# Cross-attention block on one core: the last output tile finished by column halves, and steps moved between ScalarE, VectorE and SyncE in the first and last batch

## The chip, the core and the metric

One NeuronCore of one Trainium2 chip. The metric is the device time of one execution in microseconds (us); lower is better. TensorE (PE) multiplies matrices into the accumulator banks (PSUM), VectorE (DVE), ScalarE (ACT) and GpSimd (POOL) work elementwise, and SyncE (SP) and ScalarE issue DMAs.

## The reference

```
x: (16, 100, 640)   ctx: (16, 722, 384) = enc (718 rows) + ca (4 rows)
query = x @ Wq;  keyt = enc @ Wk;  valt = enc @ Wv
hs = mha(query, keyt, valt)                      # 8 heads of 80
ca_q1 = einsum('btc,th->bch', ca, Wq_ca)[:, picked 100 rows]
ca_hs1 = mha(ca_q1, x, x)
ca_hs2 = mha(ca_hs1 @ Wq, ca @ Wk_ca, ca @ Wv_ca)
out = (hs + ca_hs2) @ Wout + b_out + x
```

Everything is float32. The kernel splits each operand of a product into a high and a low part in a type that TensorE takes at full rate and adds three products (high x high, high x low, low x high). So nearly every result comes as a pair of steps: ScalarE writes the high part (`..._high`), VectorE or GpSimd the low part (`..._low`), which is the value less its high part.

## The kernel before

The program has four stretches, and the order of the work in each is written out by hand, engine by engine; the engines meet in semaphores only. Each engine takes its own list in order, so an instruction that waits holds up all that stands behind it.

1. **Prologue.** `first_queries`, then `query(g, j)` for four column groups of x and `m_parts`, 40 small products per head and column block, written between the queries. `m_parts` for head h waits for the low part of that head's Wq (`head_low(h)`, semaphore hlo). VectorE makes them in order behind `weight_low(5, ...)`, the low part of Wk. SP's list issues the loads and the stores: `store_q` and `store_g` write the queries of group 0 back to DRAM, and the load of Wk stood behind them.
2. **`batch(0, first=True)`**, which has the queries of group 3 (`query(3, 0..5)`) written between its own steps. They all use one PSUM bank, `psB[:, 1]`, so `query(3, j)` waits for `q_low(3, j - 1)`. ScalarE also makes the high parts of Wv in it (`wv_high(0..2)`), and GpSimd subtracts them (`wv_low`).
3. **`batch(i)` for i = 1 to 14** in a loop, and `batch(15, last=True)`, which has no keys of a next batch and starts the output product instead: `tile(0, 0)`.
4. **The output tiles.** `tile(r, j)` makes 128 rows of out in 30 matmuls of 320 columns, in two column halves. 1600 rows are 12 tiles of 128 and one of 64, the last. `high(r, j)` (ACT) and `low(r, j)` (DVE) prepare its operand. `finish(r, j)` (DVE) adds the bias and the residual x, and `store(r, j)` (ACT) writes the rows out.

A batch on TensorE is, per head h: `scores` (product with the keys), `turn(h)` (transposes of the probabilities) and, per column block, `context(i, u)`. On VectorE `rowmax`, then ScalarE's `expo`, then `norm(i, h)` on VectorE, which scales the probabilities of a head by one over their sum: a reciprocal (L1593), a short copy of 39 columns (L1595) and the 718 columns themselves (L1599). `turn(i, h)` waits for `norm(i, h)` and for `pt_low(i, h - 1)`. `c2_copy`, `b2_less_max2` and `b2_norm2` (L1687 writes P2x) belong to the second, small attention, whose last transpose, `b2_turn2`, is L915.

Of the kernel before, what the change touches and what calls it, by code (L numbers as in the profile page):

```python
# [13 lines left out]
HEADS = 8  # L14
# [81 lines left out]
def program(nc, x, xT, encT, encN, caT, asel, Wq, WqT, Wk, Wv, WqcaBD, Wkca, Wvca, Wout, bout, out,  # L96
            q_d, g_d, v2_d, m_d, hs_d):

    with ExitStack() as ctx:
# [234 lines left out]
        with nc.Block() as block:  # L334
            @block.sync
            def _(sp):
# [401 lines left out]
            def _(pe):  # L738
# [179 lines left out]
                def tile(r, j, n=128, first=False):  # L918

                    pe.wait_ge(s["clo"], 2 * r + j + 1)  # L920
                    if first:
                        pe.wait_ge(s["wolo"], FT)
                        pe.wait_ge(s["exp"], HEADS * B)
                    else:
                        pe.wait_ge(s["csum"], 2 * r + j - 1)
# [7 lines left out]
                    mm.then_inc(s["cmm"], 1)  # L933
# [110 lines left out]
                def batch(i, first=False, last=False):  # L1044
# [120 lines left out]
            def _(act):  # L1165
# [10 lines left out]
                def pt_high(i, h, first=False):  # L1176
# [3 lines left out]
                    if first and h == 4:  # L1180
# [4 lines left out]
                        psT[0:KP, :, 0:3 * S].rearrange("p a (k n) -> p a k n", k=3), ACT.Copy).then_inc(s["pthi"], 1)  # L1185

# [159 lines left out]
                def batch(i, first=False, last=False):  # L1346
# [42 lines left out]
                    if first:  # L1389
                        q_high(3, 4)  # L1390
# [6 lines left out]
                    if first:  # L1397
                        xm_copy(i)
                        expo(i, 5)
# [25 lines left out]
                    if last:  # L1425
                        wo_high(3)
                        wo_high(4)
                        u_high(i, 0)
# [8 lines left out]
                    if first:  # L1437
                        wv_high(0)
                    b2_exp2(i)
                    if last:  # L1440
                        high(0, 0, first=True)
# [3 lines left out]
                    if first:  # L1445
                        wv_high(1)
# [4 lines left out]
                    if first:  # L1451
                        wv_high(2)
                    pt_high(i, 7)
                    if not last:
                        k_high(i + 1, 2)
                    if last:
# [123 lines left out]
                store(FULL // 2, 0, REST)  # L1580
                act.wait_ge(s_st[0], 16 * (FULL // 2 + 1))
# [3 lines left out]
            def _(dve):  # L1585
# [5 lines left out]
                def norm(i, h):  # L1591
# [8 lines left out]
                                            None, ALU.mult).then_inc(s["norm"], 1)  # L1600

# [101 lines left out]
                def finish(r, j, n=128, first=False):  # L1703
                    dve.wait_ge(s["cmm"], 2 * r + j + 1)
# [285 lines left out]
```

## Time and profile before

| | |
|---|---|
| device time, median of 3 runs | 985.36 us (984.73 to 988.87) |
| the profiled execution | 982.17 us |
| its span, first to last instruction | 980.5 us |
| PE busy in the span | 962.7 us (98%) |
| DVE, ACT, POOL busy | 708.7, 491.8, 343.5 us |
| granted PE clock, mean | 0.998 |

The busy times are sums over the span. PE is at work nearly all the time, so what it waits for, where, and how long, is what the profile has to answer; the times of the other engines matter only where PE waits for them.

### The profile page before, as it was taken

The numbers are of one execution on the slowest core, as the hardware profiler recorded it, in microseconds if no ns is written. First come the engines' busy times: TensorE is split into PE (matmuls) and PEld (weight loads), VectorE is DVE, ScalarE is ACT, GpSimd is POOL, SyncE is SP. The second block draws the span as 40 slices with busy tenths as digits, with TensorE's granted clock in tenths as the row PEclk, the third lists the DMA queues.
The fourth block names the chain that finished last, engine by engine and source line by source line (L and its number), as shares of the span: only waits on it lengthen the run. The fifth ranks groups of instructions, "written<-read, shape, count | busy, mean of one in ns | idle before, by whom it ended". The sixth has DMA issues, their size and how long they took to land.

```text
span 980.5 us, 21024 instructions
## 1 busy us (share of the span) xinstructions
PE 962.7 (98%) x6644; PEld 942.8 (96%) x6644; DVE 708.7 (72%) x1257; ACT 491.8 (50%) x911; POOL 343.5 (35%) x302
## 2 busy tenths in 40 slices
PE   9999989999999999999999999999999999998998
PEld 8998889999999999999999999999999999998997
DVE  6455687777777778787777877777777777777444
ACT  6434545455555546464646363736464545455110
POOL 5223353434342516161615252433433433424000
PEclk9999999999999999999999999999999999999999
DMA  7899967797979787978797979787887878795364
GB/s 264 267 294 267 291 158 209 179 212 175 210 178 203 185 200 187 191 192 193 198 186 199 189 196 183 209 188 200 184 212 166 223 168 212 177 226 156 102 193 141
DMA packets 157545, 195.21 MB, mean 199 GB/s; under 512 B 81040, under 2 KB 111568, under 8 KB 157520
## 3 DMA queue, kind: packets, MB, share of 16 engines
q1 hardware_dynamic: 150000, 181.53, 75.4%
q10 hardware_dynamic: 7520, 13.35, 4.5%
q8 instruction: 15, 0.25, 0.1%
q14 instruction: 10, 0.08, 0.0%
HBM read 82.74 MB, written 19.95 MB: 105 GB/s over the span
## 4 chain that ended last, share of the span: by engine, by line
PE 87%; DVE 5%; DMA 4%; ACT 2%; SPq 1%; issue 0%; ACTq 0%
PE psS L780 22%; PE psB L815 17%; PE psB L820 9%; PE psS L755 8%; PE psT L796 6%; PE psS L930 6%; PE psT L848 4%; PE psT L854 2%; PE psB L825 2%; PE psB L827 2%; DMA g_split<-PT_l 1%; PE psB L880 1%; PE psB L903 1%; PE psT L855 1%; PE psB L965 1%; DVE probs L1599 1%
## 5 line engine op out<-in xcount | busy, mean ns | idle before, releaser
L780 PE MATMUL psS<-encT_keep,Wk_keep 128*128 128x360 f32 x1440 | 254.1, 330 | 0.0
L780 PEld LDWEIGHTS psS<-encT_keep,Wk_keep 128*128 128x128 f32 x1440 | 237.8, 189 | 0.7
L1172 ACT ACTIVATE probs<-psS,negmax 100x718 f32<-100x718 f32 x128 | 110.2, 861 | 132.7 <-DVE negmax L1588 132.6
L815 PE MATMUL psB<-PT_h,encN_h 128*128 128x400 f32 x480 | 169.5, 353 | 0.0
L815 PE MATMUL psB<-PT_l,encN_h 128*128 128x400 f32 x480 | 165.7, 345 | 0.0
L635 POOL TENSOR_TENSOR encT_keep<-encT_raw,encT_keep 128x718 fp32r<-128x718 f32 x45 | 83.5, 1856 | 170.1 <-ACT encT_keep L1201 165.5
L1605 DVE TENSOR_TENSOR PT_l<-psT,PT_h 128x600 fp32r<-128x600 f32 x128 | 99.5, 777 | 38.3 <-ACT PT_h L1183 35.0
L626 POOL TENSOR_TENSOR Mbd<-Mbd,fmask 128x320 fp32r<-128x320 f32 x48 | 43.1, 898 | 220.1 <-DMA Mbd<-m_split 217.5
L1588 DVE TENSOR_REDUCE negmax<-psS 100x1 f32<-100x720 f32 x128 | 114.6, 895 | 0.1
L1599 DVE TENSOR_SCALAR probs<-probs,inv 100x718 f32<-100x718 f32 x128 | 106.6, 833 | 4.5
L1183 ACT ACTIVATE PT_h<-psT 128x600 fp32r<-128x600 f32 x128 | 85.7, 669 | 44.8 <-PE psT L796 42.4
L820 PE MATMUL psB<-PT_h,encN_l 128*128 128x400 f32 x480 | 103.8, 346 | 0.5 <-POOL encN_l L650 0.5
L1621 DVE TENSOR_TENSOR UT<-psB,UT 128x400 fp32r<-128x400 f32 x96 | 55.0, 573 | 64.7 <-ACT UT L1225 64.7
L1196 ACT ACTIVATE kT<-psS 128x718 fp32r<-128x718 f32 x80 | 61.6, 770 | 79.3 <-PE psS L780 76.6
L1225 ACT ACTIVATE UT<-psB 128x400 fp32r<-128x400 f32 x96 | 48.2, 502 | 92.1 <-PE psB L827 92.1
L1616 DVE TENSOR_TENSOR kT<-psS,kT 128x718 fp32r<-128x718 f32 x80 | 72.0, 900 | 27.4 <-ACT kT L1196 26.1
L815 PEld LDWEIGHTS psB<-PT_h,encN_h 128*128 128x128 f32 x480 | 90.4, 188 | 0.4
L815 PEld LDWEIGHTS psB<-PT_l,encN_h 128*128 128x128 f32 x480 | 90.5, 188 | 0.0
L796 PE MATMUL psT<-ident,probs 100*128 100x100 f32 x768 | 87.0, 249 | 2.8 <-DVE PT_l L1605 2.2
L820 PEld LDWEIGHTS psB<-PT_h,encN_l 128*128 128x128 f32 x480 | 88.1, 188 | 1.1 <-POOL encN_l L650 1.1
L755 PE MATMUL psS<-kstack,qstack_h 120*100 120x360 f32 x256 | 87.9, 343 | 0.3 <-DMA kstack<-kT 0.3
L796 PEld LDWEIGHTS psT<-ident,probs 100*128 100x128 f32 x768 | 79.3, 140 | 7.9 <-issue 2.8
(253 smaller groups left out, 1791.9 us busy)
## 6 DMA issues: line engine op xcount, KB each, us to landing
kstack<-kT SPq DMA_DIRECT2D x64, 448.8 KB
kstack<-kT SPq DMA_DIRECT2D x192, 112.2 KB
enc_raw<-in_encN_dram SPq DMA_DIRECT2D x48, 384.0 KB, 4.6
encT_raw<-in_encT_dram SPq DMA_DIRECT2D x45, 359.0 KB, 5.1
kstack<-kT SPq DMA_DIRECT2D x32, 359.0 KB
kstack<-kT SPq DMA_DIRECT2D x32, 269.2 KB
kstack<-kT SPq DMA_DIRECT2D x32, 179.5 KB, 3.6
kstack<-kT SPq DMA_DIRECT2D x64, 89.8 KB, 3.9
```

Of the source, the lines that this page charges most:

```text
L635: nc.gpsimd.tensor_tensor(eT[1][:, c, :], rawT[:, c, :], eT[0][:, c, :], ALU.subtract).then_inc(s["encT"], 1)
L755: mm = pe.matmul(psS[score_slot[h]][0:S, half, 0:HALF], qst[p][:, h, :], kst[:, p, h % SLOTS, k0:k0 + HALF], start=(p == 0), stop=(p == 1))
L780: mm = pe.matmul(keys_in(f, first)[:, half, 0:HALF], w[:, c, f * 128:(f + 1) * 128], e[:, c, k0:k0 + HALF], start=(j == 0), stop=(j == 3 * ...
L796: mm = pe.transpose(psT[0:KP, k // 3, (k % 3) * S:(k % 3 + 1) * S], P[h % PRING][0:S, k * KP:(k + 1) * KP], ident[0:S, 0:S])
L815: pe.matmul(psB[:, 1, 0:RH], eN[0][:, k, cc], PT[p][:, k, rows], start=(k == 0 and p == 0), stop=False)
L820: pe.matmul(psB[:, 1, 0:RH], eN[1][:, k, cc], PT[0][:, k, rows], start=False, stop=False)
L1172: nc.scalar.activation(halves(P[h % PRING][0:S, 0:KEYS]), without_overlap(psS[score_slot[h]], S), ACT.Exp, bias=negmax[:, h:h + 1], accum_ ...
L1183: nc.scalar.activation(PT[0][:, :, h * S:(h + 1) * S].rearrange("p (a k) n -> p a k n", a=2), psT[0:KP, :, 0:3 * S].rearrange("p a (k n) - ...
L1588: nc.vector.tensor_reduce(negmax[:, h:h + 1], tile_in(h), AX.XY, ALU.max, negate=True).then_inc(s["negmax"], 1)
L1599: nc.vector.tensor_scalar(P[h % PRING][0:S, 0:KEYS], P[h % PRING][0:S, 0:KEYS], inv[:, h:h + 1], None, ALU.mult).then_inc(s["norm"], 1)
L1605: nc.vector.tensor_tensor(o[1], psT[0:KP, :, 0:3 * S].rearrange("p a (k n) -> p a k n", k=3), o[0], ALU.subtract).then_inc(s["ptlo"], 1)
L1616: nc.vector.tensor_tensor(halves(kT[f % 2][1][:, :]), without_overlap(keys_in(f, first), 128), halves(kT[f % 2][0][:, :]), ALU.subtract).t ...
```

## The change

Seven edits:

- Prologue, SP: the load of Wk is issued ahead of `store_q(0, ...)`, and `store_g(0)` behind the load of heads 3 to 5.
- Prologue, DVE: the sum `k2_sum` is made ahead of the two `v2` subtractions.
- First batch: `query(3, 4)` stands behind `turn(0, 3)` and `scores(0, 5)` on PE; `rowmax(0, 5)` and `expo(0, 5)` stand further forward on DVE and ACT.
- First batch, ACT: `wv_high(0)` and `wv_high(1)` stand behind `b2_pt2_high`, `wv_high(2)` behind `k_high(1, 2)`.
- Last batch: `norm(15, 5)` and `norm(15, 6)` run on ScalarE, with the scale taken from `inv`; VectorE keeps their reciprocals (`one_over`). `high(0, 0)` and `low(0, 0)` stand further forward.
- `finish` adds bias and x before it waits for the product, and adds the product then; `tile` waits for the second of these steps (cres) instead of the first (csum).
- The last tile (64 rows) signals after each column half, and is finished and stored in two halves.

```diff
                 load_heads(0, 3)
+                sp.wait_ge(s["wlo"], 4)
+                sp.dma_start(wk_raw, tiled(Wk)).then_inc(s["wkin"], 16)
                 store_q(0, 0, 3)
                 store_q(0, 3, FT)
-                store_g(0)
-                sp.wait_ge(s["wlo"], 4)
-                sp.dma_start(wk_raw, tiled(Wk)).then_inc(s["wkin"], 16)
                 sp.wait_ge(s["hlo"], 3)
                 load_heads(3, 3)
+                store_g(0)
...
-                        pe.wait_ge(s["csum"], 2 * r + j - 1)
+                        pe.wait_ge(s["cres"], 2 * r + j - 1)
...
-                    mm.then_inc(s["cmm"], 1)
+                        if half == 1 or n < 128:
+                            mm.then_inc(s["cmm"], 1)
...
                     b2_turn(i, 1)
-                    if first:
-                        query(3, 4)
-                    else:
+                    if not first:
                         context(i - 1, 5)
                     turn(i, 3)
                     scores(i, 5)
+                    if first:
+                        query(3, 4)
...
+                def norm(i, h):
+                    act.wait_ge(s["inv"], 2 * (HEADS * i + h) + 1)
+                    nc.scalar.activation(P[h % PRING][0:S, KEYS:KEYS + TH],
+                                         P[h % PRING][0:S, FULLK * KP:FULLK * KP + TH], ACT.Copy,
+                                         scale=inv[:, h:h + 1]).then_inc(s["inv"], 1)
+                    act.wait_ge(s["inv"], 2 * (HEADS * i + h) + 2)
+                    nc.scalar.activation(P[h % PRING][0:S, 0:KEYS], P[h % PRING][0:S, 0:KEYS], ACT.Copy,
+                                         scale=inv[:, h:h + 1]).then_inc(s["norm"], 1)
...
+                def one_over(i, h):
+                    dve.wait_ge(s["exp"], HEADS * i + h + 1)
+                    dve.wait_ge(s["inv"], 2 * (HEADS * i + h))
+                    nc.vector.reciprocal(inv[:, h:h + 1], total[:, h:h + 1]).then_inc(s["inv"], 1)
...
                 def finish(r, j, n=128, first=False):
-                    dve.wait_ge(s["cmm"], 2 * r + j + 1)
                     if not first:
                         dve.wait_ge(s_st[j], 16 * r)
                     v = [halves(t[0:n, 0:H]) for t in (res[j], bias, xin[j])]
-                    nc.vector.tensor_tensor(v[0], psS[j][0:n, :, 0:HW], v[1], ALU.add).then_inc(s["csum"], 1)
+                    dve.wait_ge(s_x[j], 16 * r + 16)
+                    nc.vector.tensor_tensor(v[0], v[1], v[2], ALU.add).then_inc(s["csum"], 1)
                     dve.wait_ge(s["csum"], 2 * r + j + 1)
-                    dve.wait_ge(s_x[j], 16 * r + 16)
-                    nc.vector.tensor_tensor(v[0], v[0], v[2], ALU.add).then_inc(s["cres"], 1)
+                    if n == 128:
+                        dve.wait_ge(s["cmm"], 2 * r + j + 1)
+                        nc.vector.tensor_tensor(v[0], psS[j][0:n, :, 0:HW], v[0], ALU.add).then_inc(s["cres"], 1)
+                    else:
+                        for half in range(2):
+                            dve.wait_ge(s["cmm"], 2 * r + j + 1 + half)
+                            nc.vector.tensor_tensor(v[0][:, half, :], psS[j][0:n, half, 0:HW], v[0][:, half, :],
+                                                    ALU.add).then_inc(s["cres"], 1)
```

The other moves have no line that says more than the list. Three places of the order:

SP's queue in the prologue, from the load of Wv_ca on (`probs<-in_WqT_dram` are the heads' rows of Wq, `encT_raw<-in_Wk_dram` is Wk):

```order
 L424 DMA probs<-in_WqT_dram 80x3x640
+L463 DMA encT_raw<-in_Wk_dram 128x3x640
 L435 DMA q_split<-PT_h 128x3x400
 L435 DMA q_split<-PT_l 128x3x400
 L435 DMA q_split<-PT_h 128x2x400
 L435 DMA q_split<-PT_l 128x2x400
+L424 DMA probs<-in_WqT_dram 80x3x640
 L442 DMA g_split<-PT_h 64x400
 L442 DMA g_split<-PT_l 32x400
-L466 DMA encT_raw<-in_Wk_dram 128x3x640
-L424 DMA probs<-in_WqT_dram 80x3x640
```

Wk moved ahead of six stores, the heads ahead of two.

ScalarE at the end of the first batch, before (from `pt_high(0, 5)`; `Wv_h` is written by `wv_high`, `P2T` by `b2_pt2_high`, `kT` by `k_high`):

```order
L1183 ACTIVATE PT_h<-psT 128x6x100
L1324 ACTIVATE Wv_h<-encT_raw 128x640
L1253 ACTIVATE P<-P 100x32
L1196 ACTIVATE kT<-psS 128x718
L1324 ACTIVATE Wv_h<-encT_raw 128x640
L1183 ACTIVATE PT_h<-psT 128x6x100
L1257 ACTIVATE P2T<-psB 96x100
L1324 ACTIVATE Wv_h<-encT_raw 128x640
L1183 ACTIVATE PT_h<-psT 128x6x100
L1196 ACTIVATE kT<-psS 128x718
```

and of the change:

```order
L1184 ACTIVATE PT_h<-psT 128x6x100
L1263 ACTIVATE P<-P 100x32
L1206 ACTIVATE kT<-psS 128x718
L1184 ACTIVATE PT_h<-psT 128x6x100
L1267 ACTIVATE P2T<-psB 96x100
L1334 ACTIVATE Wv_h<-encT_raw 128x640 x2
L1184 ACTIVATE PT_h<-psT 128x6x100
L1206 ACTIVATE kT<-psS 128x718
L1334 ACTIVATE Wv_h<-encT_raw 128x640
```

The first Wv copy stands four instructions later, the last one behind the keys' high part.

ScalarE in the last batch, before (from the copy of hs; `Wk_keep<-encT_raw` is `wo_high`, the high part of Wout, `UT` is `u_high(15, 0)`):

```order
L1230 ACTIVATE hs<-psT 80x400
L1262 ACTIVATE Wk_keep<-encT_raw 128x640 x2
L1225 ACTIVATE UT<-psB 128x4x100
L1183 ACTIVATE PT_h<-psT 128x6x100
L1172 ACTIVATE probs,total<-psS,negmax 100x718
```

and of the change:

```order
L1240 ACTIVATE hs<-psT 80x400
L1190 ACTIVATE probs<-probs,inv 100x39
L1194 ACTIVATE probs<-probs,inv 100x718
L1272 ACTIVATE Wk_keep<-encT_raw 128x640 x2
L1190 ACTIVATE probs<-probs,inv 100x39
L1194 ACTIVATE probs<-probs,inv 100x718
L1235 ACTIVATE UT<-psB 128x4x100
L1184 ACTIVATE PT_h<-psT 128x6x100
L1173 ACTIVATE probs,total<-psS,negmax 100x718
```

Four instructions came in ahead of the copy of UT.

## Rows read from the trace of the kernel before

In rows of busy time stand start:end and length in us, then busy us (and instructions) of PE, PEld (TensorE's weight loads), DVE, ACT and POOL, the granted PE clock (1.00 is full), the DMA engines' busy share and GB/s.

**Rows 1.** Busy time of each engine by stretch of the span

```profile
0.00:60.00 60.00, 56.14 (x343) 53.68 (x344) 32.08 (x46) 32.39 (x56) 24.98 (x41) 0.97 0.87 273
60.00:140.00 80.00, 73.55 (x447) 69.14 (x447) 50.44 (x87) 38.33 (x72) 27.37 (x23) 1.00 0.88 248
140.00:880.00 740.00, 739.99 (x5207) 729.35 (x5206) 572.74 (x1045) 394.83 (x737) 276.57 (x229) 1.00 0.83 195
880.00:906.00 26.00, 23.15 (x170) 21.48 (x169) 19.62 (x37) 15.20 (x32) 14.59 (x10) 1.00 0.58 168
```

**Rows 2.** Timeline of PE, prologue: start, us, what [idle before and its releaser]

```profile
30.37 1.50 PE L1039 MATMUL psS<-kstack,P1T 80*128 80x64 f32 x12 [0.57 <-issue]
...
42.21 1.52 PE L1039 MATMUL psS<-kstack 80*128 80x64 f32 x12 [1.19 <-DVE kstack L1743]
```

**Rows 3.** Busy time and clock behind that gap

```profile
45.00:49.00 4.00, 4.00 (x18) 3.98 (x16) 0.12 (x1) 0.26 (x1) 3.69 (x5) 0.57 0.84 250
```

**Rows 4.** Chain of waits, prologue: start, us, what

```profile
29.91 7.50 DMA encT_raw<-in_Wk_dram
...
37.43 1.82 ACT Wk_keep L1294
...
39.27 2.16 DVE Wk_keep L1732
```

**Rows 5.** Timeline of PE, first batch

```profile
111.11 0.42 PE L965 MATMUL psB<-encN_h,Wv_h 128*128 128x400 f32 x1 [1.41 <-DVE PT_l L1737]
...
133.06 0.29 PE L915 MATMUL psB<-ident,P2x 100*96 100x100 f32 x1 [1.12 <-DVE P2x L1687]
...
138.25 0.71 PE L796 MATMUL psT<-ident,probs 100*128 100x100 f32 x6 [1.90 <-DVE PT_l L1605]
```

**Rows 6.** Timeline of DVE, end of the first batch

```profile
131.44 1.57 DVE L1687 TENSOR_TENSOR P2x<-P,st 100x96 f32<-100x96 f32 x1
...
133.11 1.50 DVE L1595 TENSOR_SCALAR probs<-probs,inv 100x39 f32<-100x39 f32 x1
134.64 1.96 DVE L1599 TENSOR_SCALAR probs<-probs,inv 100x718 f32<-100x718 f32 x1
```

**Rows 7.** Timeline of GpSimd, same place

```profile
131.35 4.85 POOL L672 TENSOR_TENSOR Wv_l<-encT_raw,Wv_h 128x640 fp32r<-128x640 f32 x3
```

**Rows 8.** Timeline of DVE, last batch

```profile
890.23 1.96 DVE L1599 TENSOR_SCALAR probs<-probs,inv 100x718 f32<-100x718 f32 x1
...
895.30 1.65 DVE L1599 TENSOR_SCALAR probs<-probs,inv 100x718 f32<-100x718 f32 x1
...
898.62 0.26 DVE L1687 TENSOR_TENSOR P2x<-P,st 100x96 f32<-100x96 f32 x1
...
898.98 0.24 DVE L1595 TENSOR_SCALAR probs<-probs,inv 100x39 f32<-100x39 f32 x1
899.26 0.59 DVE L1599 TENSOR_SCALAR probs<-probs,inv 100x718 f32<-100x718 f32 x1
```

**Rows 9.** Timeline of PE, last batch

```profile
893.67 0.73 PE L796 MATMUL psT<-ident,probs 100*128 100x100 f32 x6 [0.55 <-DVE P L1665]
...
900.65 0.41 PE L930 MATMUL psS<-Wk_keep,kT 128*128 128x320 f32 x1 [1.54 <-DVE kT L1700]
```

**Rows 10.** Timeline of ACT, last batch

```profile
888.82 1.36 ACT L1262 ACTIVATE Wk_keep<-encT_raw 128x640 fp32r<-128x640 f32 x2
891.24 0.50 ACT L1225 ACTIVATE UT<-psB 128x400 fp32r<-128x400 f32 x1 [1.06 <-PE psB L827]
...
894.47 0.86 ACT L1172 ACTIVATE probs<-psS,negmax 100x718 f32<-100x718 f32 x1 [2.04 <-DVE negmax L1588]
```

**Rows 11.** Timeline of DVE, end of the program

```profile
975.88 0.82 DVE L1708 TENSOR_TENSOR encT_raw<-psS,enc_raw 64x640 f32<-64x640 f32 x1 [2.71 <-PE psS L930]
976.73 0.82 DVE L1711 TENSOR_TENSOR encT_raw<-encT_raw 64x640 f32<-64x640 f32 x1
```

**Rows 12.** A DVE operation of half that width, by line: count, busy, mean ns

```profile
L1871 DVE TENSOR_TENSOR qstack_l<-psS,qstack_h 64x320 fp32r<-64x320 f32 x2 | 0.9, 471 | 0.0
```

More of the change, by code:

```diff
@@ L1389, in batch @@
                     if first:
+                        expo(i, 5)
                         q_high(3, 4)
@@ L1425, in batch @@
                     if last:
+                        norm(i, 5)
                         wo_high(3)
                         wo_high(4)
+                        norm(i, 6)
                         u_high(i, 0)
@@ L1436, in batch @@
                     pt_high(i, 5)
-                    if first:
-                        wv_high(0)
+                    if last:
+                        high(0, 0, first=True)
                     b2_exp2(i)
                     if last:
-                        high(0, 0, first=True)
                         u_high(i, 1)
@@ L1451, in batch @@
                     if first:
-                        wv_high(2)
+                        wv_high(0)
+                        wv_high(1)
                     pt_high(i, 7)
@@ L1455, in batch @@
                         k_high(i + 1, 2)
+                    if first:
+                        wv_high(2)
                     if last:
@@ L1579, in _ @@
                 store(FULL // 2 - 1, 1)
-                store(FULL // 2, 0, REST)
-                act.wait_ge(s_st[0], 16 * (FULL // 2 + 1))
+                for half in range(2):
+                    act.wait_ge(s["cres"], FULL + 1 + half)
+                    act.dma_start(out2[FULL * 128:NT, half * HW:(half + 1) * HW],
+                                  res[0][0:REST, half * HW:(half + 1) * HW]).then_inc(s_st[0], 16)
+                act.wait_ge(s_st[0], 16 * (FULL // 2 + 2))
                 act.wait_ge(s_st[1], 16 * (FULL // 2))
@@ L1785, in batch @@
                     b2_pt_low(i, 1)
+                    if first:
+                        rowmax(i, 5)
                     norm(i, 4)
@@ L1791, in batch @@
                     if first:
-                        rowmax(i, 5)
                         xm_add(i)
@@ L1806, in batch @@
                         xm_low(i)
+                    if last:
+                        one_over(i, 5)
                     if not first:
                         hs_add(i - 1, 1)
-                    norm(i, 5 if first or last else 6)
+                    if last:
+                        one_over(i, 6)
+                    else:
+                        norm(i, 5 if first else 6)
                     if last:
@@ L1816, in batch @@
                     rowmax(i, 7)
-                    if first or last:
+                    if first:
                         norm(i, 6)
@@ L1822, in batch @@
                     pt_low(i, 5)
+                    if last:
+                        low(0, 0)
                     b2_norm2(i)
@@ L1825, in batch @@
                     if last:
-                        low(0, 0)
                         u_low(i, 1)
@@ L1867, in _ @@
                 head_low(2)
+                dve.wait_ge(s["k2hi"], 3)
+                k2_parts = psB[0:D, :, :].rearrange("d b (h a n) -> d b h a n", h=4, a=2)
+                k2_sum4 = k2_sum.rearrange("d (b h n) -> d b h n", b=2, h=4)
+                nc.vector.tensor_tensor(k2_sum4, k2_parts[:, :, :, 0, :], k2_sum4, ALU.add).then_inc(s["k2lo"], 1)
                 for j in range(2):
```

8 lines of the change are left out of this document (1 added, 7 removed).

## The prediction

> **What bounds the kernel now.** I read the busy times by stretch first, because they say where TensorE stands still. From 140 to 880 us, the fourteen looped batches, PE is busy for 739.99 of 740 us [rows 1]: nothing can be gained there, and whatever PE is early by at 140 it keeps, unless a wait comes up that was not there. The other stretches have all the slack there is: 3.86 us in the first 60 us, 6.45 us from 60 to 140, 2.85 us from 880 to 906 [rows 1], and what follows the last product. So I went through PE's timeline in these stretches, gap by gap, and for each gap through the timeline of the engine that released it, and in the prologue the chain of waits.
>
> In the prologue PE waits 0.57 us ahead of the first small products and 1.19 us ahead of those of head 3 [rows 2]. The chain behind the second: the load of Wk starts at 29.91 and takes 7.50 us, ScalarE's copy of it starts at 37.43, VectorE's subtraction runs 2.16 us from 39.27, and only then comes the head's low part [rows 4]. A little after that gap the granted clock falls: over 45 to 49 us its mean is 0.57 with PE busy all the time [rows 3], 4.00 x 0.43 = 1.72 us of work lost at the lower of the two rates (1.2 instead of 2.4 GHz).
>
> In the first batch PE waits 1.41 us for `query(3, 4)`, 1.12 us for P2x and 1.90 us for `turn(0, 7)` [rows 5]. The last two have one source: on VectorE the P2x step takes 1.57 us, the short copy 1.50 and the long one 1.96 us [rows 6], where the same three take 0.26, 0.24 and 0.59 us late in the last batch [rows 8]. During the slow ones GpSimd runs the three Wv subtractions, 4.85 us from 131.35 on [rows 7]. In the last batch the same long copy takes 1.96 and 1.65 us [rows 8], and PE waits 0.55 us for `c2_copy` and 1.54 us for `low(0, 0)` [rows 9].
>
> **The change part by part.**
>
> *Prologue.* Wk's load needs `weight_low(4)`, done about when SP issues its first store, and then has the 2 MB of query stores behind it instead of ahead. With its 7.50 us [rows 4] kept it lands near 31 instead of 37.4; then heads 3 to 5, issued some 3 us earlier, decide. Head 3's low part was ready at about 42.2, the moment PE goes on [rows 2], and now is ready some 3 to 4 us earlier, so the 1.19 us gap closes. The bound from the other side: if the DMA engines are so full that the heads land as late as before, Wk's 1.82 and 2.16 us are at least out of the line, and about 1 us remains. `store_g(0)` lands later; `q_high(1, 0)` waits for it, but stands behind head 3 on ScalarE anyway. `k2_sum` ahead of two subtractions of 0.47 us [rows 12] brings the last `k2` step forward by about 0.45 of the 0.57 us. If the gap is gone I take the slow clock to be gone too: 0.45 + 1.19 + 1.72 = 3.36 us, between 1.0 and 3.36.
>
> On this last term the Trainium skill, page "TensorE: Matmul & The Clock Gate", Part 1, says that idling brings the slow rate on and that the watch over activity runs freely and does not restart with the kernel, so that one kernel shows different numbers of slow matmuls from run to run. By that rule this stretch may stay although the gap closes, and the sum would be 1.7 us less; or other gaps pay for one in other runs.
>
> *First batch, `query(3, 4)`.* It cannot start before `q_low(3, 3)`, at 111.11 [rows 5], wherever it stands. The transposes and scores, ten short matmuls of some 1.2 us, now fill the wait ahead of it, and no longer stand between it and `query(3, 5)`, which has to wait for `q_low(3, 4)`: about 1.4 us from the end of one to the start of the next, with some 0.8 us of `b2_xm` in it. So 1.2 us gained, 0.6 to 0.7 paid again: net 0.5 us, between 0.2 and 1.2.
>
> *First batch, Wv.* GpSimd's subtractions cannot start before the high parts, which now follow `b2_pt2_high`, 2.3 us later. By then P2x and the two copies of `norm(0, 7)` are through: 1.31 + 1.26 + 1.37 = 3.94 us shorter on VectorE [rows 6, 8]. The P2x gap of 1.12 goes to 0.0 to 0.1; `pt_low(0, 6)` is then done 0.5 us before PE comes to `turn(0, 7)`, so the 1.90 goes too: 3.0 us. What is late next is GpSimd: its last subtraction ends about 139.3 on the old scale, and PE, now 3.2 us ahead, wants Wv at 140.4. That is 1.1 us of cover; each further us of delay costs one.
>
> *Last batch.* VectorE's work between `hs_add` and `u_low` falls by both norms' copies. On ScalarE a copy with a scale read per row is not in the trace; the nearest row, the exponential with a bias read per row on the same 718 columns, takes 0.86 us [rows 10]. The short one lies between nothing and that; I take 0.3. Each pair holds ScalarE some 1.1 us, less overlap. With the two Wout copies of 1.36 us [rows 10] between them, the copy of UT, which started at 891.24 [rows 10], starts about 892.3, and `pt_high`, `pt_low` and `c2_copy` follow it: the 0.55 us gap [rows 9] grows to about 1.35. Behind it VectorE has no `norm` left and `low(0, 0)` is ready at 898.3, while PE is there at 899.2: the 1.54 us gap [rows 9] closes, and a short one before `turn(15, 6)`. So tile 0 starts at 899.2 instead of 900.65: 1.4 us gained; 0.5 if the copies take 0.4 us more each than I think.
>
> *Output tiles.* In all but the last tile there is still one VectorE step between the product and the release of its bank, so PE sees no change. The bias and x sum now waits for x before the bank is released, but x is loaded a whole tile ahead. At the end two steps follow the last matmul, from 975.88 to 977.55 [rows 11]. Now only one of half the width does: a half-width operation took 0.471 us [rows 12]. 1.69 - 0.49 = 1.2 us gained. The first half's store is hidden behind the matmuls.
>
> Sum: 3.36 + 0.5 + 3.0 + 1.4 + 1.2 = 9.5 us. The profiled execution took 982.17, so 972.7 us like that one. The median of the runs is 985.36, 3.2 us above it; I put the same gain there: 985.4 - 9.5 = 975.9.
>
> **The rivals.** A difference under 0.5% (4.9 us) is about what a measurement of this kernel can't tell from none.
>
> 1. *The prologue's gain is not kept* (the heads land as before, or the slow clock comes anyway). For it: the DMA share is 0.87 in the first 60 us and 0.88 in the next 80 [rows 1], so transfers crowd. Against it: PE released nearly all that followed in the old chain. Price: 1.7 to 2.4 us, so 977.6 to 978.3.
> 2. *The copies stay stretched, or Wv comes late.* A Wv subtraction takes a third of 4.85, 1.62 us [rows 7], and a stretched copy 1.26 to 1.37 us more than a free one [rows 6, 8], as if it waited out most of one. If the first subtraction starts before `norm(0, 7)` is through, one copy waits, and PE by up to 1.6 us; or GpSimd is the one held up, and PE waits for Wv before the loop. Up to 3.0 us lost: 978.9. The margin is 0.9 us by the rows. The Trainium skill, page "SBUF — State Buffer", section "SBUF: two separate sides", has a rule for it: the port pair that VectorE and GpSimd share is an exclusive lock, held by whoever starts first for its whole instruction.
> 3. *Both, or most of prologue and first batch absorbed before 140 us.* Then 2.6 to 4 us are left: 981.4 to 982.8, within the noise.
> 4. *More than forecast.* The unprofiled runs are 2.6 to 6.7 us slower than the profiled one. If that is one or two more slow-clock stretches at the gaps of the first batch, they go with the gaps: 1.7 or 3.4 us more, 972.5 to 974.2.
> 5. *Slower.* `csum`, which opens `finish`, now waits for the load of x, and the bank's release stands behind it. If that load landed late, PE would wait at each of some nine tiles. An x load is issued a little over 4 us before VectorE could use it and the bank is wanted a tile (4.4 us) after that. To undo 9.5 us and cost 5 more, each would have to be late by 1.6 us beyond both margins: 990. It decides when a load takes over about 8 us.
>
> **How the numbers follow.** Forecast 0.47, rival 1 0.18, rival 2 0.10, rival 4 0.09, rival 3 0.13, rival 5 0.03. The first four, 0.84, end under 980.4 and are "faster by over 0.5%"; the third 0.13, "within"; the fifth 0.03, "slower". The likeliest case gives 975.9. The range leaves out the far half of rival 4, most of rival 3's upper end and rival 5: 972 to 981.5.
>
> **What would show it.** In the profile after: no gap before head 3's products and no lower clock between 40 and 50 us; Wk's copy on ScalarE near 30 instead of 37.43; P2x, short and long copy at the end of the first batch near 0.26, 0.24 and 0.59; GpSimd's Wv steps starting after them and PE not waiting for Wv; PE starting tile 0 about 9 us earlier than 900.65, with a longer wait before the `turn` that follows `c2_copy`; two scaled copies on ScalarE near 0.9 us; one half-width step of 0.47 us after the last matmul. The prediction is wrong if the stretch from 140 on starts less than 4 us earlier than before, or if a new wait stands at the start of the loop.

## The result, and the profile after

| | before | after |
|---|---|---|
| median of 13 runs each | 984.73 us (980.34 to 989.39) | 975.57 us (971.92 to 980.56) |
| ratio | | 0.9909, 95% interval 0.9890 to 0.9928 |
| the profiled execution, its span | 982.17, 980.5 us | 975.57, 973.9 us |

The changed kernel is 9.2 us faster by the medians; 9.5 had been forecast. The profiled executions are only 6.6 us apart.

Busy time by stretch of the changed kernel, columns as in [rows 1]:

```profile
0.00:60.00 60.00, 58.27 (x354) 56.01 (x355) 34.16 (x49) 34.60 (x60) 24.76 (x41) 0.97 0.88 275
60.00:140.00 80.00, 76.58 (x458) 72.27 (x456) 48.44 (x90) 37.23 (x69) 27.47 (x23) 0.98 0.92 257
140.00:880.00 740.00, 740.00 (x5210) 729.18 (x5210) 571.35 (x1045) 397.46 (x742) 278.36 (x230) 1.00 0.83 194
...
33.00:37.00 4.00, 4.00 (x17) 3.97 (x16) 0.08 (x1) 0.13 (x1) 0.00 (x0) 0.57 1.06 313
94.00:99.00 5.00, 4.50 (x16) 4.46 (x17) 3.41 (x5) 2.05 (x5) 0.00 (x0) 0.66 0.88 224
```

PE's idle time fell from 3.86 to 1.73 us in the first 60 us and from 6.45 to 3.42 us in the next 80. The last two rows are what the forecast's sum had not counted and rival 1 had named. The lower clock, the 1.2 GHz level, which stood at 45 to 49 us [rows 3], is at 33 to 37 now and again at 94 to 99. Each costs 4.00 x 0.43 or 5.00 x 0.34, about 1.7 us.

PE's timeline, the gaps of the first and the last batch:

```profile
82.15 0.38 PE L755 MATMUL psS<-kstack,qstack_h 120*100 120x360 f32 x1 [0.59 <-DMA kstack<-kT]
93.04 0.41 PE L755 MATMUL psS<-kstack,qstack_h 120*100 120x360 f32 x1 [0.81 <-DVE kT L1636]
...
111.53 0.42 PE L966 MATMUL psB<-encN_h,Wv_h 128*128 128x400 f32 x1 [0.44 <-DVE PT_l L1763]
115.79 0.91 PE L939 MATMUL psB<-encN_h,v2bd 128*64 128x400 f32 x4 [0.47 <-DVE PT_l L1763]
...
131.50 0.27 PE L915 MATMUL psB<-ident,P2x 100*96 100x100 f32 x1
134.64 0.68 PE L796 MATMUL psT<-ident,probs 100*128 100x100 f32 x6
...
891.01 0.73 PE L796 MATMUL psT<-ident,probs 100*128 100x100 f32 x6 [1.46 <-DVE P L1685]
895.71 0.39 PE L930 MATMUL psS<-Wk_keep,kT 128*128 128x320 f32 x1
```

Against [rows 5, 9]: 1.41 us became 0.44 and a new 0.47; the gaps of 1.12, 1.90 and 1.54 us are gone; 0.55 grew to 1.46. VectorE at the end of the first batch, and the first two of GpSimd's three Wv steps:

```profile
131.17 0.26 DVE L1707 TENSOR_TENSOR P2x<-P,st 100x96 f32<-100x96 f32 x1
...
131.53 0.24 DVE L1610 TENSOR_SCALAR probs<-probs,inv 100x39 f32<-100x39 f32 x1
131.81 0.59 DVE L1614 TENSOR_SCALAR probs<-probs,inv 100x718 f32<-100x718 f32 x1
...
133.43 3.22 POOL L672 TENSOR_TENSOR Wv_l<-encT_raw,Wv_h 128x640 fp32r<-128x640 f32 x2 [2.42 <-ACT Wv_h L1334]
```

The three steps have the lengths of [rows 8] instead of those of [rows 6], and GpSimd starts behind them. ScalarE in the last batch with the two copies that it took over, and VectorE at the end of the program:

```profile
885.28 0.32 ACT L1190 ACTIVATE probs<-probs,inv 100x39 f32<-100x39 f32 x1
885.63 0.90 ACT L1194 ACTIVATE probs<-probs,inv 100x718 f32<-100x718 f32 x1
...
888.83 0.48 ACT L1235 ACTIVATE UT<-psB 128x400 fp32r<-128x400 f32 x1
```

```profile
967.33 0.81 DVE L1728 TENSOR_TENSOR encT_raw<-enc_raw,encT_raw 64x640 f32<-64x640 f32 x1
968.78 0.48 DVE L1736 TENSOR_TENSOR encT_raw<-psS,encT_raw 64x320 f32<-64x320 f32 x1 [0.64 <-PE psS L930]
970.91 0.48 DVE L1736 TENSOR_TENSOR encT_raw<-psS,encT_raw 64x320 f32<-64x320 f32 x1 [1.65 <-PE psS L930]
```

Where the 6.6 us lie, by the starts of the same instructions on PE:

| | before | after | ahead by |
|---|---|---|---|
| `keys(0, 0)`, the first key product | 62.20 | 60.32 | 1.88 |
| `keys(1, 0)` | 118.43 | 118.29 | 0.14 |
| `b2_turn2` of batch 0 | 133.06 | 131.50 | 1.56 |
| `b2_turn2` of batch 1 | 186.12 | 182.62 | 3.50 |
| tile 0 | 900.65 | 895.71 | 4.94 |
| last matmul | 975.53 | 970.56 | 4.97 |
| end of the span | 980.5 | 973.9 | 6.6 |

Between 60 and 118 us the lead was lost again: 1.71 us to the second slow stretch (a stretch at the lower clock), 0.7 us to waits that vary from run to run, against the 0.7 us that `query(3, 4)` gave.

### The profile page after: what moved, and what is told of

It reads as the page before. It is cut to its first block, busy times and chain, and to the rows that moved or that the text cites. A ratio compares the mean times of both kernels' runs of the same rounds, so it can differ in the third digit from the quotient of the medians.

```text
span 973.9 us, 21030 instructions
## 1 busy us (share of the span) xinstructions
PE 963.8 (99%) x6644; PEld 944.6 (97%) x6644; DVE 700.7 (72%) x1254; ACT 494.4 (51%) x915; POOL 342.3 (35%) x302
## 4 chain that ended last, share of the span: by engine, by line
PE 91%; DVE 2%; ACT 2%; DMA 2%; SPq 1%; POOL 1%; issue 1%; ACTq 0%; POOLq 0%
PE psS L780 24%; PE psB L815 18%; PE psB L820 9%; PE psS L755 8%; PE psT L796 6%; PE psS L930 6%; PE psT L848 4%; PE psT L854 2%; PE psB L966 2%; PE psB L825 2%; PE psB L827 2%; PE psS L1040 1%; PE psB L880 1%; PE psB L903 1%; PE psT L855 1%; PE psT L966 1%
## 5 line engine op out<-in xcount | busy, mean ns | idle before, releaser
L635 POOL TENSOR_TENSOR encT_keep<-encT_raw,encT_keep 128x718 fp32r<-128x718 f32 x45 | 83.6, 1858 | 177.6 <-ACT encT_keep L1211 173.2
L1614 DVE TENSOR_SCALAR probs<-probs,inv 100x718 f32<-100x718 f32 x126 | 101.2, 803 | 4.4
L1206 ACT ACTIVATE kT<-psS 128x718 fp32r<-128x718 f32 x80 | 61.7, 771 | 83.6 <-PE psS L780 76.4
```

The costliest lines, as they stand in the source:

```text
L635: nc.gpsimd.tensor_tensor(eT[1][:, c, :], rawT[:, c, :], eT[0][:, c, :], ALU.subtract).then_inc(s["encT"], 1)
L1614: nc.vector.tensor_scalar(P[h % PRING][0:S, 0:KEYS], P[h % PRING][0:S, 0:KEYS], inv[:, h:h + 1], None, ALU.mult).then_inc(s["norm"], 1)
```

## The experiments

Twelve more kernels ran, the changed one again among them, in three sets, each on one chip beside the kernel before. Each run also lists its mean granted clock.

| kernel | runs | median, us | ratio to before (95%) | mean clock |
|---|---|---|---|---|
| before, set 1, 2, 3 | 35, 29, 17 | 985.00, 983.94, 984.89 | | 0.9953, 0.9963, 0.9959 |
| after, the first runs (beside 13 of before, 984.73) | 13 | 975.57 | 0.9909 (0.9890 to 0.9928) | 0.9979 |
| e1_prologue (set 1) | 12 | 984.37 | 0.9993 (0.9970 to 1.0015) | 0.9959 |
| e2_wv (1) | 12 | 983.19 | 0.9984 (0.9966 to 1.0002) | 0.9951 |
| e3_last (1) | 12 | 984.43 | 0.9990 (0.9968 to 1.0012) | 0.9954 |
| e5_gp (1) | 12 | 981.15 | 0.9975 (0.9952 to 0.9998) | 0.9957 |
| after_again (2) | 6 | 976.25 | 0.9933 (0.9909 to 0.9957) | 0.9983 |
| e6_one_piece (2) | 12 | 978.62 | 0.9943 (0.9921 to 0.9965) | 0.9968 |
| e7_norm6 (2) | 12 | 976.69 | 0.9934 (0.9909 to 0.9958) | 0.9977 |
| e9_g2 (2) | 12 | 978.49 | 0.9941 (0.9921 to 0.9961) | 0.9970 |
| e10_two (3) | 6 | 979.54 | 0.9946 (0.9924 to 0.9967) | 0.9977 |
| e12_first (3) | 12 | 982.09 | 0.9972 (0.9955 to 0.9988) | 0.9959 |
| e11_old_q34 (3) | 6 | 978.09 | 0.9923 (0.9897 to 0.9949) | 0.9962 |
| e14_best (3) | 6 | 976.81 | 0.9919 (0.9892 to 0.9946) | 0.9975 |

A part of the change is worth one to three us, and an interval is some 4 us wide. So each part is read from the trace, stretch by stretch, and the times serve as a check. Where the clock's share is said to be taken off a time, that is the time less (1 - clock) x span, run by run, and the means are compared.

**e1_prologue: the prologue's edits alone.**

```diff
+                sp.wait_ge(s["wlo"], 4)
+                sp.dma_start(wk_raw, tiled(Wk)).then_inc(s["wkin"], 16)
                 store_q(0, 0, 3)
...
                 load_heads(3, 3)
+                store_g(0)
```

> The kernel before with the two prologue edits alone (load of Wk ahead of the query stores, store_g(0) behind the heads, k2_sum earlier). Theory A, the gain is the closed waits and nothing else: the gaps of 0.57 and 1.19 us on TensorE are gone, what follows stands 1.8 to 1.9 us earlier, and a stretch of lower clock, some 3.4 us long, still comes somewhere in the first 100 us, since the changed kernel showed two of them with the gap closed: 1.8 us less than before. Theory B, as the prediction had it, the lower clock belongs to the gap before head 3: no stretch below full clock in the first 60 us, 3.4 us less than before. Theory C, the early load of Wk crowds out the later transfers and the gain is paid back before 140 us: 0 to 0.5 us less than before, with longer waits for kstack's rows or for the keys' high part between 80 and 95 us.

Both gaps are gone and the first key product starts at 58.70, 1.8 us earlier than before's with its slow stretch taken off. The stretch of lower clock that theory A also expected in the first 100 us did not come; this trace has none before its end. But PE's timeline has this further on, which is what theory C had named:

```profile
82.08 0.38 PE L755 MATMUL psS<-kstack,qstack_h 120*100 120x360 f32 x1 [1.76 <-DMA kstack<-kT]
```

By tile 0 nothing of the lead is left: 899.23 against 900.65 - 1.71 = 898.94 before. By the times the edits gave 0.6 us, and 0.4 with the clock's share taken off. In e10_two beside e12_first, which differ by the same edits, it is 2.6 us by the medians and 0.6 with that share off. What they are worth beside the clock is within the noise of the times; it takes several traces. The first key product, each slow stretch ahead of it taken off at 1.71 us, starts on average at 58.9 in the nine traces with these edits (58.6 to 59.3) and at 60.05 in the five without them (59.5 to 60.5): 1.1 us. At `keys(0, 3)`, near 84 us, it is still 1.0 (83.6 against 84.6). The wait of 1.76 us is this trace's alone: the other eight with the edits have 0 to 0.6 us there, the five without 0 to 0.65. The gap before head 3 is 1.19 us in [rows 2], but 0.89, 0.65 and 0.25 us in e2_wv, e3_last and e12_first, and e5_gp's timeline has none. Theory A holds for the closed gaps, not for the size. Theory C's longer wait does not repeat; how much of the 1.1 us the program keeps to its end no run settles. Theory B fits this one trace and falls by the others: with the gap closed the low clock still came ahead of 38 us in five of the nine traces, both of the changed kernel's among them; of the five without the edits two have it ahead of 50 us.

**e2_wv and e12_first: Wv alone, and the first batch alone.** e2_wv moves only the Wv copies; e12_first has `query(3, 4)`, `rowmax(0, 5)` and `expo(0, 5)` at their new places as well.

```diff
-                    if first:
-                        wv_high(0)
                     b2_exp2(i)
...
                     b2_pt2_high(i)
+                    if first:
+                        wv_high(0)
+                        wv_high(1)
```

> The kernel before with wv_high(0..2) moved to their new places and nothing else. Theory A, the three long copies on VectorE were held up by GpSimd's Wv subtractions beside them: P2x step, short copy and long copy take 0.26, 0.24 and 0.59 us, the gaps of 1.12 and 1.90 us on TensorE go, nothing waits for Wv, 3.0 us less than before. Rival, the gain belongs to TensorE being 2.4 us ahead through the other edits: with Wv moved alone a Wv subtraction still meets one of the copies, one of them stays above 1.3 us, and 1 to 2 us are gained.

> The kernel before with the first batch's edits alone (Wv and query(3, 4) with rowmax and expo). Theory A, Wv alone had given 2.1 us behind P2x, with 0.97 us of a new wait ahead of turn(0, 6) in place of the 1.12 us for P2x, since norm(0, 6) now met GpSimd's next two steps full on (1.25 and 1.92 us in place of 0.38 and 1.64); query(3, 4) gives 0.7 and moves that meeting: 2.8 us less than before if norm(0, 6) is still met full on, 3.5 to 4 if not. Rival, the two edits don't touch each other: 0.7 + 2.1 = 2.8 with the wait of 0.97 unchanged.

In e2_wv the three steps take 0.26, 0.25 and 0.60 us and the gap before `turn(0, 7)` is gone, but only 2.1 us are gained: the wait for P2x came back one transpose earlier. PE, VectorE and GpSimd of e2_wv:

```profile
131.68 0.71 PE L796 MATMUL psT<-ident,probs 100*128 100x100 f32 x6 [0.97 <-DVE PT_l L1604]
```

```profile
126.54 1.25 DVE L1594 TENSOR_SCALAR probs<-probs,inv 100x39 f32<-100x39 f32 x1
127.83 1.92 DVE L1598 TENSOR_SCALAR probs<-probs,inv 100x718 f32<-100x718 f32 x1
```

```profile
126.51 1.24 POOL L620 TENSOR_TENSOR xTb_l<-P,xTb_h 128x500 fp32r<-128x500 f32 x1
127.83 1.52 POOL L602 TENSOR_TENSOR gbd<-g_in,headmask 128x800 fp32r<-128x800 f32 x1
```

`norm(0, 6)` met two other GpSimd steps full on: the short copy ends 0.04 us behind the first of them, the long one 0.40 us behind the second. In the kernel before it met these steps at another phase, with 0.38 and 1.64 us. In e12_first the same copies take 0.25 and 1.65 us, no wait stands at `turn(0, 6)`, and from `keys(1, 0)` to `b2_turn2` of batch 1 it takes 64.57 us, against 67.69 before and 65.57 in e2_wv. With the 0.7 us of `query(3, 4)` that is 3.8 us, as theory A had it for a norm that is not met full on; the times say 2.8 us, with an interval of 1.2 to 4.4.

That it is `query(3, 4)` which avoids the meeting is not shown. e11_old_q34 has it at its old place and avoids the meeting too: 0.47 and 1.65 us, no wait, 64.31 us for the stretch. e6_one_piece and e9_g2 have it at the new place and meet GpSimd all but full on, with waits of 0.67 and 0.81 us ahead of `turn(0, 6)`. VectorE in e9_g2:

```profile
125.43 1.09 DVE L1610 TENSOR_SCALAR probs<-probs,inv 100x39 f32<-100x39 f32 x1
126.56 1.92 DVE L1614 TENSOR_SCALAR probs<-probs,inv 100x718 f32<-100x718 f32 x1
```

So `query(3, 4)` is worth 0.7 us, and up to 1 us of the gain of the Wv edit hangs on a phase that varies from trace to trace and that these runs don't trace to one edit.

**e5_gp: GpSimd held back, ScalarE left alone.**

```diff
                 spread_g(1)
+                pool.wait_ge(s["norm"], HEADS)
                 wv_low()
```

> The kernel before with one more wait: GpSimd begins its three Wv subtractions only when the first batch's last norm(0,7) is done; ScalarE's copies of Wv stay where they were. Theory A, GpSimd's subtractions are what stretches VectorE's three steps: they take 0.26, 0.24 and 0.59 us here too, the gaps of 1.12 and 1.90 us go; with nothing paid back 3.0 us less than before, and up to 1 us of it paid if TensorE then waits for Wv. Rival, ScalarE's copies of Wv beside them, or the traffic of transfers, stretches them: they stay at 1.3 to 2.0 us and the time is that of before.

VectorE and GpSimd:

```profile
131.10 0.26 DVE L1688 TENSOR_TENSOR P2x<-P,st 100x96 f32<-100x96 f32 x1
...
131.47 0.25 DVE L1596 TENSOR_SCALAR probs<-probs,inv 100x39 f32<-100x39 f32 x1
131.75 0.60 DVE L1600 TENSOR_SCALAR probs<-probs,inv 100x718 f32<-100x718 f32 x1
```

```profile
132.49 4.85 POOL L672 TENSOR_TENSOR Wv_l<-encT_raw,Wv_h 128x640 fp32r<-128x640 f32 x3 [2.93 <-ACT Wv_h L1325]
```

ScalarE's copies of Wv still run beside the three steps and do no harm. GpSimd's steps were the cause; the rival falls. With one wait more the program is 3.85 us faster by the medians; in the trace it gains the same 2.1 us in this stretch as e2_wv and has, likewise, 0.95 us of wait ahead of `turn(0, 6)`.

**e3_last: the last batch alone.**

```diff
+                        norm(i, 5)
                         wo_high(3)
                         wo_high(4)
+                        norm(i, 6)
                         u_high(i, 0)
```

> The kernel before with the edits of the last batch alone (heads 5 and 6 normalised on ScalarE, high(0,0) and low(0,0) further forward). Theory A: the gap before low(0,0)'s tile (1.54 us) goes, the one behind c2_copy grows from 0.55 to 1.4 to 1.5 us, tile 0 starts 1.4 us earlier measured from the gap of 0.42 us at the start of this batch; 1.4 us less than before, too small for the time alone to tell. Rival, the 1.4 us in the changed kernel came in part from its being 3.5 us ahead of the loads: then under 0.7 us here.

From the small gap of 0.42 us at the start of this batch to tile 0 it takes 13.88 us (887.65 to 901.53), against 15.19 before (885.46 to 900.65) and 13.79 in the changed kernel. 1.3 to 1.4 us, with the gap behind `c2_copy` at 1.37: theory A. The times alone, 0.6 us less, could not have told.

**after_again.**

> The changed kernel once more, on the chip and in the rounds of the next three. Its first 13 runs had a mean granted clock of 0.9979, while 35 runs of the kernel before, and 48 of the kernels with one part of the change each, had 0.9951 to 0.9959. Theory A, with all the waits closed the low clock comes less often: 0.997 to 0.998 here against 0.995 to 0.996 of before beside it, 9.0 to 9.5 us less than before, of which some 6.5 to 7 us is work and waits and 2 to 2.5 us the clock. Theory B, the difference in clock belonged to the chip or the hour: both clocks within 0.0005 of each other here and 6.5 to 8.3 us less than before.

7.7 us less by the medians, clock 0.9983 against 0.9963. The clock is theory A's, the time is within theory B's bounds; the interval, 4.2 to 9.0 us, reaches into both. With the clock's share taken off it is 5.7 us, less than the 6.5 to 7 that theory A gave to work and waits. The clock's difference came again with the two kernels side by side, so chip and hour alone don't explain it. Its ScalarE and PE show a wait that the prediction had not named:

```profile
123.37 0.67 ACT L1184 ACTIVATE PT_h<-psT 128x600 fp32r<-128x600 f32 x1 [2.25 <-DMA g_split<-PT_l]
```

```profile
126.97 3.23 PE L780 MATMUL psS<-encT_keep,Wk_keep 128*128 128x360 f32 x18 [0.71 <-ACT probs L1173]
```

`pt_high(0, 4)` writes where `query(3, 5)` was kept and waits until that is stored. It did so before the change too (0.41 us). Over the thirteen traces with it the wait is 0.31 to 4.34 us, and the store takes 4.3 to 8.2 us from issue to landing. `pt_high(0, 4)` is followed on ScalarE by `expo(0, 7)`, and PE waits for that.

**e6_one_piece: the last tile in one piece, in the new order.**

```diff
-                    if n == 128:
-                        dve.wait_ge(s["cmm"], 2 * r + j + 1)
-                        nc.vector.tensor_tensor(v[0], psS[j][0:n, :, 0:HW], v[0], ALU.add).then_inc(s["cres"], 1)
-                    else:
-                        for half in range(2):
...
+                    dve.wait_ge(s["cmm"], 2 * r + j + 1)
+                    nc.vector.tensor_tensor(v[0], psS[j][0:n, :, 0:HW], v[0], ALU.add).then_inc(s["cres"], 1)
```

> The changed kernel with its last tile finished and stored in one piece; the order bias + x first, product last is kept. Of the 1.63 us that the end gained in the profile, 1.20 was VectorE's and 0.43 the store's. Theory A: behind the last product stand one step of 0.82 us and a store of 2.9 us, so the end is 0.34 + 0.43 = 0.8 us later than in the changed kernel, and the reordering alone is worth the other 0.85. Rival, the store takes 2.5 us at either size: 0.35 us later. Both are read from the last rows of the profile; the time is 0.4 to 0.8 us above that of the changed kernel.

```profile
977.18 0.81 DVE L1727 TENSOR_TENSOR encT_raw<-psS,encT_raw 64x640 f32<-64x640 f32 x1 [2.84 <-PE psS L930]
```

From that step's end, 977.99, to the end of the span of 980.9 it is 2.9 us; before, 980.5 - 977.55 = 2.95; in the changed kernel, 973.9 - 971.39 = 2.5. Theory A: of the end's 1.6 us, 0.86 come from the order of the sums (975.88 to 977.55 [rows 11] became one step of 0.81), 0.33 from the half-width step and 0.4 from the smaller store.

**e7_norm6: head 6 normalised behind `pt_high(15, 4)`.**

```diff
                         wo_high(4)
-                        norm(i, 6)
                         u_high(i, 0)
...
                     pt_high(i, 4, first)
+                    if last:
+                        norm(i, 6)
                     expo(i, 7)
```

> The changed kernel with norm(15, 6) on ScalarE behind pt_high(15, 4) instead of ahead of u_high(15, 0). Theory A, the gap of 1.46 us behind c2_copy is made by that norm standing ahead of the copy of UT, 1.2 us in ScalarE's queue: UT's copy starts about 1.1 us earlier, the gap shrinks to 0.4 to 0.5 us, tile 0 starts 1.0 us earlier, 1.0 us less than the changed kernel. Rival, head 6's normalisation is now late for turn(15, 6), or VectorE's own steps set the place of c2_copy: the gap only moves, 0 to 0.3 us gained.

```profile
894.62 0.73 PE L796 MATMUL psT<-ident,probs 100*128 100x100 f32 x6 [0.46 <-ACT probs L1194]
```

The gap is 0.46 us and tile 0 starts 12.77 us behind the 0.42 us gap instead of 13.79: 1.0 us, theory A. The profiled run lost more elsewhere, and the median is not below after_again's. ScalarE in its first batch:

```profile
126.22 0.67 ACT L1184 ACTIVATE PT_h<-psT 128x600 fp32r<-128x600 f32 x1 [4.34 <-DMA g_split<-PT_l]
```

**e9_g2: `store_g2` issued behind `k_high(0, 3)`.**

```diff
                         store_q2(4, FT)
-                        store_g2()
...
                         q_high(3, 0)
+                        store_g2()
```

> The changed kernel with store_g2 issued behind k_high(0, 3) and q_high(3, 0) instead of ahead of them. In its trace ScalarE spends 0.80 and 2.26 us issuing these two stores (0.57 and 1.25 in the kernel before), the keys' high part starts right behind them at 91.27, and TensorE waits 0.81 us for their low part. Theory A, the wait of 0.81 us is those issues': it goes, k_high stands 2 us earlier, and 0.5 to 0.8 us are gained. Rival, VectorE, which has the second attention's normalisation ahead of the low part until 91.0, sets it: the gap stays at 0.2 us as in the kernel before, and the pressure on the transfers gives another 0.3 to 1 us of wait elsewhere.

The keys' high part starts at 88.09 instead of 91.27 and the wait of 0.81 us is gone. In after_again, without the edit, it isn't there either; in e12_first it is 1.82 us, and there ScalarE's issue of the second store took longest of all the traces:

```profile
88.72 3.50 ACTq L1336 DMA_DIRECT2D g_split<-PT_l  x1
```

The same issue took 2.26 us in the changed kernel's first trace, 1.57 in after_again and 0.60 here. So the wait is the issues', as theory A had it, but it comes in some runs only. PE waits 1.22 us at 81.34 in this trace, and the median is 2.2 us above after_again's, inside the intervals. No gain is shown.

**e10_two: prologue and first batch.** The diffs of e1_prologue and e12_first together.

> The kernel before with the edits of the prologue and of the first batch, without those of the last batch and of the end. In the changed kernel's first profile TensorE stood 1.89 us ahead at the first key product of batch 0 and 3.5 us ahead behind the first batch (5.2 without a stretch of lower clock that this trace has more). Theory A, prologue and first batch add up: 5 us less than before in work and waits, and the time left over to the whole change is 3.0 us. Theory B, part of the prologue's gain is taken back before the loop, since ScalarE's pt_high(0, 4) waits for the last store of the queries to land, 0.4 to 2.3 us in every trace so far, wherever TensorE stands: 3 to 4 us less than before, and at the end of the first batch TensorE is less ahead than the sum of the two parts alone.

5.35 us less by the medians; by the trace 4.7 us, slow stretches taken off. That is nearer to theory A; the times with the clock's share taken off say 3.2 us, which is theory B's. It stays open. In its stretch from `keys(1, 0)` to `b2_turn2` of batch 1, 64.40 us, hardly anything is paid back (`pt_high(0, 4)` waited 0.93 us); in after_again the same stretch took 65.40, with 2.25 us of that wait.

**e11_old_q34: `query(3, 4)` back at its old place.** The first piece of the change's diff on PE undone, with `rowmax(0, 5)` and `expo(0, 5)`.

> The changed kernel with query(3, 4), rowmax(0, 5) and expo(0, 5) back at their old places. Theory A: the wait for q_low(3, 3) is 1.3 to 1.5 us again instead of 0.3 to 0.45, the one of 0.47 us ahead of query(3, 5) goes; 0.7 us slower than the changed kernel, and the rest of the first batch is shifted by as much. Rival, the store of the last query sets the end of the first batch in any case: no difference behind the first batch, although the wait is back.

The wait is 1.54 us again, the one of 0.47 is gone. From `keys(0, 4)` to `keys(1, 0)` it takes 20.02 us (99.59 to 119.61), against 19.41 in the changed kernel (98.88 to 118.29), 19.39 to 19.55 in the eight traces with the edit, and 20.12 before: 0.6 to 0.7 us, theory A. By the times the two can't be told apart.

**e14_best: both further edits.** Beside e7_norm6's edit:

```diff
+            if g == 3 and j == FT:
+                return g3_own[p][rows, :]
...
+        g3_own = [UT_keep[:, (4 + p) * GT:(5 + p) * GT] for p in range(2)]
...
+                    if first:
+                        act.wait_ge(s["qst3c"], 16 * 2)
                     pt_high(i, 7)
```

> The changed kernel with two more edits: norm(15, 6) behind pt_high(15, 4), as tried before, and query(3, 5) kept in a part of UT that nothing else writes until batch 1, so that pt_high(0, 4) no longer waits for its store (a wait for that store stands ahead of pt_high(0, 7) now). Theory A, that store is what the first batch ran into: pt_high(0, 4) starts 0.7 to 2.3 us earlier, no wait of keys(1, 1) for an exponential is left, and with the 1.0 us of the last batch 1.5 to 2.5 us less than the changed kernel (974 by the median). Rival, GpSimd's steps for the next batch, which clash with norm(0, 6) at another phase then, or the store of query(3, 4), set the same end: 1.0 us less, all of it in the last batch.

ScalarE and PE:

```profile
119.78 0.67 ACT L1187 ACTIVATE PT_h<-psT 128x600 fp32r<-128x600 f32 x1
```

```profile
887.67 0.73 PE L799 MATMUL psT<-ident,probs 100*128 100x100 f32 x6 [0.45 <-ACT probs L1197]
```

`pt_high(0, 4)` waits for nothing, and the stretch of the first batch takes 64.17 us, the shortest of all. The span of 970.5 us is the shortest of all the traces too, but this trace has no slow stretch, and with its two taken off the changed kernel's first has 970.5 as well. The median of six runs, 976.81 where 974 was expected, and the ratio of 0.9919 can't be told from those of the changed kernel. It beats the kernel before; that it beats the changed one isn't shown.

## Why the prediction was right, and where it was not

The time was right, 975.57 against 975.9, and most of the sum's terms were. The sum made for the profiled execution, 972.7, was not: that one took 975.57. Two errors of about the same size, 2 us, cancelled in the forecast for the median, the clock term and rival 4 below; that is luck. And by one of the prediction's own signs it was wrong: the stretch from 140 us on was to start at least 4 us earlier, and behind the first batch this trace is 3.50 us ahead (4.58 in after_again). PE was to start tile 0 about 9 us earlier; it did so by 4.94 and 3.83.

- **Prologue, 3.36 us forecast.** Both gaps closed, Wk's copy on ScalarE started at 29.08, and head 3's low part was done at 38.46, 3.4 us before PE came to it. The step that failed is "if the gap is gone I take the slow clock to be gone too": 1.72 us that did not come, as rival 1 had it. And the 1.19 us of [rows 2] was a long sample of a wait that varies. Over all traces the closed gaps are worth 1.1 us at the first key product.
- **`query(3, 4)`, 0.5 us.** 0.7; the new wait of 0.47 us was named (0.6 to 0.7).
- **Wv, 3.0 us.** 3.36 in the changed kernel's first trace, 2.3 in its second, in which the unforeseen wait for the store stood ahead of it. The cause, GpSimd beside VectorE, was right and is shown by e5_gp. Left out was that the same meeting happens at `norm(0, 6)`, and that 0.7 to 1 us of the gain hangs on it.
- **GpSimd's cover.** PE never waits for Wv; the third subtraction ends at 139.70.
- **Last batch, 1.4 us.** 1.40, with copies of 0.32 and 0.90 us (0.3 and 0.86), and a gap of 1.46 (1.35).
- **End, 1.2 us.** 1.6; VectorE's part was right (1.67, which the prediction writes 1.69, to 0.48), and the smaller store's 0.4 us was not counted.
- **What is early at 140 us stays early.** So it was in the first trace. In after_again PE's lead fell from 4.58 us behind the first batch to 3.83 at tile 0, although the last batch gave 1.4: PE waited 1.28 us for rows of kstack and 0.62 for a transfer at 881 to 888 us. Four other traces have 1.9 to 2.8 us of the first wait. The prediction had no term for it.
- **Rival 2** happened at another place than forecast, `norm(0, 6)`, in four of the eleven traces in which `norm(0, 7)` was clear: e2_wv, e5_gp, e6_one_piece and e9_g2. **Rival 5** did not: no tile waits for x.
- **Rival 4** made up for the clock term. With the clock's share taken off, the time is 980.75 us on average for the 81 runs of before in the three sets and 974.31 for the 19 of the changed kernel: 6.4 us. The plain means are 984.86 and 976.21: 8.7 us. The other 2.2 us are granted clock. Over the 67 runs of the changed kernel and its five variants the clock is 0.9974, against 0.9958 for the 81, and the four parts alone have 0.9951 to 0.9959. Prologue and first batch have 0.9959 each alone and 0.9977 together (e10_two, six runs). Rival 4 put the low clock at the gaps of the first batch; where it was lost in the runs without a trace isn't known.

What stays open is which closed wait brings the clock back. The traces show what came before a slow stretch, below, but one trace for each kernel doesn't settle the share of each gap. With the slow stretches taken off, the changed kernel's two profiled runs are 8.3 and 5.5 us ahead of before's, 6.9 on average; the times say 6.4 over all runs, and 5.7 in the one set in which both kernels list their clocks side by side. So the closed waits are worth some 6 to 7 us, less than the 7.8 of the sum without its clock term; what the change gives in a single run also depends on waits for transfers, such as the 0.31 to 4.34 us ahead of `pt_high(0, 4)`.

## What to carry to other kernels

A gap read from one trace is a sample: where its releaser is a transfer or stands behind one, look at the same gap in several runs before pricing it. When a step is moved away from another engine's work, look at what else that engine does in the new phase, since the stall may only move there. Where the parts are worth less than the interval of a measurement, add them up from the same stretch of many traces, and count the clock separately.

## What the runs showed of the hardware

- **VectorE and GpSimd.** A VectorE step that only reads and writes SBUF ends just behind the GpSimd step that it meets, the short copy 0.04 us and the long one 0.40 us behind: in e2_wv 1.25 us instead of 0.25 with a GpSimd step from 126.51 to 127.75. Steps that read PSUM keep their length beside GpSimd (the keys' low part, 0.91 us at 123.05, beside GpSimd's 3.77 us from 121.77, in e2_wv). The Trainium skill, page "SBUF — State Buffer", section "SBUF: two separate sides", says that the port pair which the two engines share is an exclusive lock, held for the whole instruction by whichever starts first; by that rule, the traces agree.
- **The clock.** In the loop from 140 to 880 us, where PE hardly waits, the 14 traces have one stretch at the lower level among them, in e6_one_piece at 474.3 us, right behind waits of 1.48 and 0.61 us. Ahead of the last batch four traces have a wait of 1.9 to 2.8 us for rows of kstack, and all four have a slow stretch that begins in it or at most 1 us behind it. Of e12_first, PE and busy time:

```profile
884.70 0.59 PE L755 MATMUL psS<-kstack,qstack_h 120*100 120x360 f32 x1 [2.37 <-DMA kstack<-kT]
```

```profile
884.00:892.00 8.00, 7.30 (x40) 7.23 (x41) 3.71 (x8) 4.06 (x10) 5.83 (x5) 0.57 0.46 120
```

  At 32 to 34 us it begins in six traces, five without and one with the 0.57 us gap of [rows 2] ahead of it; PE had just done the small products of 64 columns, as it had in the eight others. The waits of 1.9 us before `turn(0, 7)`, in three traces, brought none on, nor did the 1.76 us at 82.08 in e1_prologue. So these traces show what often stands ahead of a slow stretch, not what decides it.
- **A smaller last store.** 2.5 us from the last VectorE step to the end for 320 columns, 2.9 for 640.
- **Issuing a store.** ScalarE's issue of one and the same store of 50 KB, near 90 us, took 0.59 to 3.50 us over the fourteen traces, and in the thirteen traces in which the keys' high part stands next in its list, that starts 0.18 us behind the issue's end.
